# One product for two message parts, for two gathered tiles and for both supers of a pair, and a third part split by keys

## The reference: what is computed

```
h   = relu(layernorm(x))                      # 6250 x 64
msg = sum over r of (etype == r) * (h[src] @ weight[r])
out = x + segment_sum(msg, dst, 6250)
```

## Time and profile before

| | us |
|---|---|
| median of 3 runs (1139.3 to 1141.56) | 1141.29 |
| the profiled execution's own time | 1139.6 |
| its span, first to last instruction | 1137.9 |
| PE busy | 1105.6 (97%) |
| DVE busy | 982.7 (86%) |
| POOL busy | 712.3 (63%) |
| ACT busy | 498.1 (44%) |

### The profile page before, as it was taken

One profiled execution on the slowest core, in us unless ns is written; L12 is line 12 of the kernel. 1 busy time (PEld: TensorE's weight loads), 2 busy tenths in 40 slices (PEclk: granted clock), 3 DMA queues, 4 the chain that ended last, 5 costly groups with the idle time before them and its releaser, 6 DMA issues.

```text
span 1137.9 us, 41624 instructions
## 1 busy us (share of the span) xinstructions
PE 1105.6 (97%) x16806; PEld 689.4 (61%) x16806; DVE 982.7 (86%) x2609; ACT 498.1 (44%) x1227; POOL 712.3 (63%) x696
## 2 busy tenths in 40 slices
PE   3899999999999999999999999999999999999996
PEld 1444666666666666666666666666666666666664
DVE  7965798898898889988998998988998899899973
ACT  4866444443444344434443444434443444344441
POOL 1410577777666766777676677776666776776730
PEclk9989999999999999999999999999999999999999
DMA  6876422122222221222122221222122222221211
GB/s 187 346 282 245 159 85 77 58 84 84 78 58 84 81 85 57 78 84 84 56 79 83 84 77 60 84 82 81 57 83 83 82 59 80 79 86 60 77 46 58
DMA packets 40043, 108.99 MB, mean 96 GB/s; under 512 B 15917, under 2 KB 15919, under 8 KB 36780
## 3 DMA queue, kind: packets, MB, share of 16 engines
q1 hardware_dynamic: 13566, 55.53, 13.8%
q0 software_dynamic: 21344, 21.90, 8.2%
q10 hardware_dynamic: 4942, 28.88, 6.4%
HBM read 78.56 MB, written 27.70 MB: 93 GB/s over the span
## 4 chain that ended last, share of the span: by engine, by line
PE 94%; DMA 2%; ACT 2%; DVE 1%; issue 0%; POOL 0%; SPq 0%; ACTq 0%; DVEq 0%; POOLq 0%
PE ps L1045 50%; PE ps L1030 25%; PE ps L1067 5%; PE ps L1081 4%; PE ps L942 3%; PE ps L975 3%; PE ps L969 1%; PE ps L983 1%; PE ps L989 1%; DMA w_cat<-weight 1%; ACT u L546 1%; DVE h_sb L906 1%; DMA table<-u 1%; ACT vals L528 0%; PE ps L936 0%
## 5 line engine op out<-in xcount | busy, mean ns | idle before, releaser
L475 POOL DMA_INDIRECT u<-table,row_idx x667 | 689.4, 1034 | 344.5 <-PE ps L1045 176.5
L1045 PE MATMUL ps<-u 64*64 64x512 bf16 x9600 | 587.3, 379 | 0.0
L592 ACT CAST u<-ps 128x384 bf16<-128x384 f32 (+1 forms) x832 | 339.1, 473 | 440.9 <-PE ps L1030 433.6
L783 DVE TENSOR_SCALAR u<-iota_key,z_sb 128x512 bf16<-128x512 f16 x1600 | 495.6, 380 | 24.2 <-PE ps L1045 22.2
L1045 PEld LDWEIGHTS ps<-u 64*64 64x64 bf16 x9600 | 255.2, 106 | 233.2 <-issue 30.0
L1030 PE MATMUL ps<-parts,u 128*128 128x192 bf16 x3136 | 314.6, 247 | 0.8 <-ACT u L546 0.8
L1030 PEld LDWEIGHTS ps<-parts,u 128*128 128x128 bf16 x3136 | 249.5, 98 | 64.9 <-issue 56.5
L773 DVE TENSOR_SCALAR u<-u,node_id 128x1664 bf16<-128x1664 f16 (+2 forms) x256 | 162.7, 676 | 8.6 <-DMA u<-rel_dram 8.6
L803 DVE TENSOR_TENSOR accT<-accT,ps 128x32 f32 x240 | 44.8, 186 | 61.9 <-DVE accT L803 24.2
L601 ACT COPY u<-ps 128x512 f32<-128x512 f32 x128 | 68.8, 590 | 39.6 <-PE ps L1045 39.6
L732 DVE TENSOR_TENSOR u<-iota_slot,rank 128x896 f16<-128x896 f16 x64 | 70.0, 1094 | 2.2
(11 more groups left out here) (90 smaller groups left out, 365.7 us busy)
## 6 DMA issues: line engine op xcount, KB each, us to landing
u<-rel_dram SPq DMA_DIRECT2D x64, 800.0 KB
table<-u ACTq DMA_DIRECT2D x24, 1024.0 KB, 5.2
u<-table,row_idx POOLq DMA_INDIRECT x667
rel_dram<-rel_row SPq DMA_DIRECT2D x64, 6.2 KB
x_sb<-x SPq DMA_DIRECT2D x2, 448.0 KB
out<-h_sb SPq DMA_DIRECT2D x3, 224.0 KB
out<-h_sb ACTq DMA_DIRECT2D x3, 224.0 KB
table<-u ACTq DMA_DIRECT2D x1, 512.0 KB, 3.3
```

The lines of the kernel that those rows point to most:

```text
L475: pool.indirect_dma_start(out=msg_p[:, b, j, :], out_offset=None, in_=table, in_offset=bass.IndirectOffsetOnAxis(ap=row_idx[:, j, m:m + 1] ...
L592: act.copy(msg_s[:, u % MB, 0:width, :].rearrange("p q c -> p (q c)"), ps[gather_bank(u)][:, 0:width * ROW]).then_inc(s_gev, 1)
L783: dve.tensor_scalar(khot[:, v % KR, :], iota_key[:, :], z_sb[:, n % 3, 1, q:q + 1], None, ALU.is_equal).then_inc(s_khot, 1)
L1045: last = pe.matmul(ps[3 + a][half * D:(half + 1) * D, :], msg_s[rows, u % MB, q % 2, part * D:(part + 1) * D], khot[rows, v % KR, :], star ...
```

## The change

Four edits, of which the first three join products on PE:

1. `sum_sorted`: parts 0 and 1 of a range are one product with a stationary operand of 64 slots x 128 features (64*128), for each super. Part 2 stays 64*64: for a bank of two ranges four products, as before. For the lone range part 2 is split by keys: 256 keys to the one half, 256 to the other, so four products of 256 columns stand for two of 512.
2. `sum_gathered`: two tiles are one product of 128 edges x 128 (two tiles of 64) by 64 columns (two windows of 32), all 128*128. Only the two diagonal blocks of the result are used, so DVE adds each block's sum in two pieces of 64 rows (`add`), and the places in the bank are twice as wide.
3. `sort_permute`: both supers' slots are one stationary operand of 128 columns, 7 products of 100 columns instead of 14 of 50. ACT takes the two diagonal blocks in two copies, and DVE writes the slots' one-hot in the new order (`placed`).
4. The planner's cost of a lone range's sums goes from 2 to 1.5 rounds. The sums of gathered blocks stay where they are in PE's stream; for some tiles the PE event after which POOL fetches is another one close by.

```diff
@@ -147 +148 @@
             now += 0.14
             last_n, last_c = STREAM[i - 1]
             for b in banks_of(last_n, last_c):
-                now += 0.214 * (3 if 2 * b + 1 < SQ else 2)
+                now += 0.214 * (3 if 2 * b + 1 < SQ else 1.5)
                 marks.append((now, "agg", last_n * SQ + min(2 * b + 2, SQ)))
         now += 0.72 * (c == 0 and n > T_PAIRS)
         for us, job, which in ((0.32, permuted, "z"), (0.13, turned, "relT"), (0.7, ranked, "ranked")):
@@ -179 +180 @@
 
     batch = [place[m] // 2 for m in range(NP)]
     batches = [[m for m in range(NP) if batch[m] == k] for k in range(NPR // 2 + 1)]
-    adds_of = lambda k: GR * (k >= 1) + len(batches[k])
+    adds_of = lambda k: GR * (k >= 1) + sum(min(2, len(tiles_of(m))) for m in batches[k])
     added_by = lambda k: sum(adds_of(i) for i in range(k + 1))
 
     def target_bank(k):
         return ps[(7, 5)[k % 2]]
 
     def sum_place(m):
-        at = GR * SW + batches[batch[m]].index(m) * PW
-        return slice(at, at + PW)
-
-    assert GR * SW + max(len(ms) for ms in batches) * PW <= BANK and max(len(ms) for ms in sums_in) <= len(sum_at)
+        at = GR * SW + batches[batch[m]].index(m) * 2 * PW
+        return slice(at, at + 2 * PW)
+
+    assert GR == 4 and GR * SW + max(len(ms) for ms in batches) * 2 * PW <= BANK and max(len(ms) for ms in sums_in) <= len(sum_at)
 
 
     def gather_bank(u):
@@ -272 +273 @@
         a0 += MB * ROW
         agg = u2[:, a0:a0 + GR * KEYS].rearrange("p (s c) -> p s c", s=GR)
         a0 += GR * KEYS
-        slot_hot = u2[:, a0:a0 + PT * CAP // 2].bitcast(F16).rearrange("p (c z) -> p c z", z=CAP)
+        slot_hot = u2[:, a0:a0 + PT * CAP // 2].bitcast(F16).rearrange("p (j z) -> p j z", j=SJ)
 
 
         u3 = sb("u3", [P, TRING * 2 * RD])
@@ -554 +555 @@
                 if g >= 3:
                     act.wait_ge(s_khot, (g - 2) * SQ)
                     act.wait_ge(s_relT, g - 2)
-                act.copy(z_sb[:, g % 3, :, :].rearrange("p v q -> p (v q)"), ps[6][:, 0:2 * SQ]).then_inc(s_zev, 1)
+                for a in range(2):
+                    rows = slice(a * CAP, (a + 1) * CAP)
+                    act.copy(z_sb[rows, g % 3, :, :].rearrange("p v q -> p (v q)"),
+                             ps[6][rows, a * 2 * SQ:(a + 1) * 2 * SQ]).then_inc(s_zev, 1)
 
             def take_rel(g):
                 act.wait_ge(s_relT, g + 1)
@@ -720 +724 @@
                 qids = qid_t[:, 2 * g:2 * g + 2, :].rearrange("p s j -> p (s j)")
                 dve.tensor_tensor(ranges[:, :, :], spread(qids, SQ), repeat(iota_range[:, :], PT), ALU.is_equal).then_inc(s_ranges, 1)
 
+            def placed(hots, first, ranks, n):
+
+                there = hots[:, :, :].rearrange("p j (a z) -> p a j z", a=2)
+                places = iota_slot[:, first:first + n].rearrange("p (a j z) -> p a j z", a=1, j=1).to_broadcast([P, 2, SJ, n])
+                mine = ranks.rearrange("p (a j z) -> p a j z", j=SJ, z=1).to_broadcast([P, 2, SJ, n])
+                return dve.tensor_tensor(there, places, mine, ALU.is_equal)
+
             def sort_slots(g):
 
                 dve.wait_ge(s_ranked, g + 1)
@@ -729 +740 @@
                 step(dve.tensor_reduce(rank[:, g, :], ranks[:, :, :], AX, ALU.add))
                 if g >= 1:
                     dve.wait_ge(s_z, g)
-                dve.tensor_tensor(slot_hot[:, :, :], repeat(iota_slot[:, 0:CAP], PT), spread(rank[:, g, :], CAP),
-                                  ALU.is_equal).then_inc(s_slots, 1)
+                placed(slot_hot, 0, rank[:, g, :], CAP).then_inc(s_slots, 1)
 
             def sort_values(g):
                 if g == 0:
@@ -775 +785 @@
                 last.then_inc(s_hot, 1)
 
             def key_hots(n, low, high):
-                dve.wait_ge(s_zev, n + 1)
+                dve.wait_ge(s_zev, 2 * (n + 1))
                 for q in range(low, high):
                     v = n * SQ + q
                     if v >= KR:
@@ -796 +806 @@
 
                 bank = target_bank(k)
 
-                def add(rows, base, width, at):
+                def add(base, *places):
+
                     if added[0]:
                         dve.wait_ge(s_add, added[0])
-                    here = accT[rows, bass.ds(base, width)]
-                    dve.tensor_tensor(here, here, bank[rows, at], ALU.add).then_inc(s_add, 1)
-                    added[0] += 1
+                    for rows, at in places:
+                        here = accT[rows, bass.ds(base, at.stop - at.start)]
+                        dve.tensor_tensor(here, here, bank[rows, at], ALU.add).then_inc(s_add, 1)
+                        added[0] += 1
 
                 if k == 1:
                     dve.wait_ge(s_acc0, 8)
@@ -821 +833 @@
                         base_row[0:1, NS + batches[k][0]:NS + batches[k][-1] + 1], engines=[dve.engine], min_val=0, max_val=N,
                         skip_runtime_bounds_check_because="the bases are clamped to it where they are made")
                     for m, base in zip(batches[k], bases):
-                        add(slice(0 if len(tiles_of(m)) > 1 else tiles_of(m)[0] % 2 * D, P), base, PW, sum_place(m))
+                        at = sum_place(m).start
+                        add(base, *[(slice(half * D, (half + 1) * D), slice(at + half * PW, at + (half + 1) * PW))
+                                    for half in range(0 if len(tiles_of(m)) > 1 else 1, 2)])
 
             dve.wait_ge(s_turn_s, 6)
             source_hots(0, 0)
@@ -978 +992 @@
             def sort_permute(g):
                 pe.wait_ge(s_slots, g + 1)
                 pe.wait_ge(s_vals, g + 1)
+
+                values = spreadv[:, :, :, :].rearrange("p (a j) v q -> p a j (v q)", j=SJ)
                 for j in range(SJ):
-                    for a in range(2):
-                        last = pe.matmul(ps[6][a * CAP:(a + 1) * CAP, 0:2 * SQ], slot_hot[:, a * SJ + j, :],
-                                         spreadv[:, a * SJ + j, :, :].rearrange("p v q -> p (v q)"), start=j == 0, stop=j == SJ - 1)
+                    last = pe.matmul(ps[6][:, 0:4 * SQ].rearrange("p (a c) -> p a c", a=2), slot_hot[:, j, :], values[:, :, j, :],
+                                     start=j == 0, stop=j == SJ - 1)
                 last.then_inc(s_z, 1)
 
             def sort_turn(g):
-                pe.wait_ge(s_zev, g + 1)
+                pe.wait_ge(s_zev, 2 * (g + 1))
                 pe.transpose(ps[6][0:SQ, 0:P], z_sb[:, g % 3, 0, :], ident[:, :]).then_inc(s_relT, 1)
 
             piece(0)
@@ -1038 +1053 @@
                 if n >= 1 and c == 0:
                     pe.wait_ge(s_aev, 2 * n)
 
-                def sums(q, part, half):
+                def sums(q, first, last, half, keys=slice(0, KEYS), stop=False):
                     u, v = n * GB + q // 2, n * SQ + q
                     for a in range(2):
                         rows = slice(a * CAP, (a + 1) * CAP)
-                        last = pe.matmul(ps[3 + a][half * D:(half + 1) * D, :], msg_s[rows, u % MB, q % 2, part * D:(part + 1) * D],
-                                         khot[rows, v % KR, :], start=q == 0 and part < 2,
-                                         stop=(q, part) in ((SQ - 1, 1), (SQ - 1, 2)))
-                    return last
+                        done = pe.matmul(ps[3 + a][half * D:(half + last - first) * D, keys],
+                                         msg_s[rows, u % MB, q % 2, first * D:last * D], khot[rows, v % KR, keys],
+                                         start=q == 0 and first == 0, stop=stop)
+                    return done
 
                 for b in banks_of(n, c):
                     both = range(2 * b, min(2 * b + 2, SQ))
                     pe.wait_ge(s_gev, n * GB + b + 1)
                     for q in both:
                         pe.wait_ge(s_khot, n * SQ + q + 1)
-                        sums(q, 0, 0)
-                        sums(q, 1, 1)
-                    for q in both:
-                        sums(q, 2, q % 2).then_inc(s_agg, 1)
+                        sums(q, 0, 2, 0)
+                    if len(both) == 2:
+                        for q in both:
+                            sums(q, 2, 3, q % 2).then_inc(s_agg, 1)
+                    else:
+                        sums(q, 2, 3, 0, slice(0, KEYS // 2), True)
+                        sums(q, 2, 3, 1, slice(KEYS // 2, KEYS), True).then_inc(s_agg, 1)
 
             def weigh(g):
                 k = g + 1
@@ -1075 +1093 @@
                 pe.wait_ge(s_gp[m % PRING], 16 * fetched(m))
                 if added_by(batch[m] - 2) > 0:
                     pe.wait_ge(s_add, added_by(batch[m] - 2))
-                tiles = tiles_of(m)
-                for j in tiles:
-                    rows, half = rows_of(m, j), j % 2
-                    last = pe.matmul(target_bank(batch[m])[half * D:(half + 1) * D, sum_place(m)], msg_p[rows, m % PRING, j, :],
```

(16 more changed lines are left out.)

## The result

The changed kernel takes 1321.9 us, median of 4 runs (1320.7 to 1322.54), against 1140.99 us for the kernel before in the same sitting: a ratio of 1.1587, 95% interval [1.1567, 1.1607]. It is slower by 180.9 us. The profiled execution took 1320.7 us with a span of 1318.9.

What follows compares the result with a forecast made beforehand. PE was taken to bound the kernel (97% busy, 94% of the chain). 1139.6 + 145.6 (sum_sorted) + 37.4 (sum_gathered) + 0 (sort_permute, fetches) = 1322.6, taken as 1319 us for rounding; range 1272 to 1365.

Steps and rivals of the forecast that it cites:

- The three terms: sum_sorted on PE: lone range's half round -6.9 us, changes into 64*64 +61.0, changes into 64*128 +91.5; together +145.6.
- the unknown one: sum_sorted: 832 new changes into 64*128 bf16 sums, taken at 0.11 us each, +91.5 us; bounds nothing and 0.20 each.
- the 58 ns between the means of the fp32 loads: sum_gathered: fp32 loads of 128 columns against 64 (195, 137 ns) pace the passes, 0.66 us a block instead of 0.35.
- the third rival: sum_sorted: wide 64-row bf16 loads are slow like L942's, 0.20 us into each 64*128 group; 1394 to 1398 us, chance 0.08.
- up to 36 was allowed for the adds: DVE: 111 more adds at 0.32 us from start to start, +36 us on an engine with 155 us to spare.
- 3.6 for rounding: Forecast's sum: 1322.6 lowered to 1319 us, since prices come from two-decimal rows; 0.005 less on each of 1340 is 7.
- The second: PE's changes of shape: one costs only where the row split changes; 1170 us, chance 0.05.
- The fourth: sum_gathered: the fp32 loads are hidden or no slower, so that edit costs nothing; 1282 us, chance 0.10.
- the fifth: sum_sorted: the two wide products don't run side by side, 1600 rounds more, +346; 1665 us, chance 0.02.
- The first: PE's small products: paced by the instruction, changes without a late producer free; 1114 us, faster, chance 0.04.

Runs made afterwards that it cites:

- e6: All sums 64*128, the second range's part 2 left out and the first range's part 1 added twice, against the kernel before: 1133.52 us, ratio 0.9943.
- e5: Only the sum_sorted edit, but in each chunk all 64*128 products first, then all 64*64, against the kernel before: 1167.0 us, ratio 1.0239.
- e7: Only the sum_gathered edit, with 32 moving columns instead of 64 (second tile's own sums left out), against the kernel before: 1182.71 us, ratio 1.0376.
- e4: Only the lone range's part 2 split by keys, all products 64*64, against the kernel before: 1301.04 us against 1293.09, ratio 1.005.
- e8: Only the sum_sorted edit, lone range's split included, run once more against the kernel before: 1300.14 us against 1291.3, ratio 1.0068.
- e2: Only the sum_gathered edit, in the first sitting, against the kernel before: 1282.01 us against 1293.09, ratio 0.9892.
- e3: Only the sort_permute edit (both supers in one product of 128 columns) against the kernel before: 1282.95 us against 1293.09, ratio 0.9894.
- e9: Only the sum_gathered edit, all 64 moving columns, run once more against the kernel before: 1281.67 us against 1291.3, ratio 0.9922.
- e11: The sum_gathered and sort_permute edits together, sums as before, against the kernel before: 1278.95 us against 1291.3, ratio 0.9898.
- e10: Only the lone range's part 2 split by keys, run once more against the kernel before: 1299.75 us against 1291.3, ratio 1.0059.
- e12: Lone range's split, and four chunks instead of five from the third pair on, sums 64*64, against the kernel before: 1301.06 us against 1290.94, ratio 1.0064.

## Why the prediction was right

It gave 1319 us with a range of 1272 to 1365; 1321.9 was measured.

**The bound** is PE before and after: the chain's 94% and 95%.

**Edit 1** was put at +145.6. By the chain a pair past the second takes 3 x 0.56 + 0.34 + 0.23 = 2.25 more, x 62 = 139.5, and the first two pairs about 4 more at the same prices: 143.5. The three terms: the rounds stay (e6: 2.05 against 2.07 for nine), so does the price of a change into 64*64; the unknown one, into 64*128 bf16, was taken as 0.11 and is 0.105 by e6. That it is a change of shape which costs, and not a slow wide product, is shown by e5: the same products, 0.46 us less a chunk with four changes fewer. The loads show what the time is: no load is made ahead over the change. By the Trainium skill's rule in "TensorEngine Tiling (Array Packing)", Key Properties, a change of mode drains the array; the trace agrees, with 0.115 us, and also where only the column width changes within 64 rows.

**Edit 2** was put at +37.4: measured 0.33 a block x 111 = 36.6. The term's reason, the 58 ns between the means of the fp32 loads, is borne out by e7, where half the moving columns left 1.46 of 1.48 us. It rests on something that the prediction didn't say: before, the two loads of a pair ran side by side, so a pair cost the time of one load. The Trainium skill's figure for a load in "TensorE: Matmul & The Clock Gate", LDWEIGHTS, about 107 ns for 128 columns by estimate, fits this pace of 0.11 a pass; for wide bf16 loads the trace denies it (mean 94 against 103 for the narrow ones). That was the third rival, and it fell: the pieces of 64*128 take 0.53 us, not 0.63.

**Edit 3** was put at nothing: +0.09 x 64 and -0.11 x 63 are -1.2. ACT's two copies were covered; DVE's busy time rose by 17 us where up to 36 was allowed for the adds.

**Edit 4** left nothing to see on the chain, and was not run alone.

The terms as measured add to 143.5 + 36.6 - 1.2 = 178.9, the spans differ by 1318.9 - 1137.9 = 181.0. Added over the whole chain, the sums are 144.2 longer, the gathered sums 36.7, the permute 6.1, the gather 7.7 shorter, together 179.3; the rest lies in pieces of the other engines. The forecast was 179.4 above before, 183.0 less 3.6 for rounding. That it came so near is in part luck: its terms were 4 too high (edit 1 by 2, edits 2 and 3 by 1 each), the 3.6 is about half of the 7 that it gave for rounding, with no reason for that half, and the 2 us of the other engines were in no term.

**The rivals.** The second (no cost within one row split) would have shown 0.43 for the first piece; it takes 0.53, and the chain's 2.63 for three banks is 3 x (0.105 + 0.12) + 9 x 0.216 = 2.62. The fourth (hidden fp32 loads) and the fifth (wide products one after another, 0.97 for the first piece) are excluded by 1.48 and 0.53. The first, time by the instruction, is wrong for this comparison, and e6 shows it: half as many products in each bank, 0.02 us a chunk. In the other sittings the ratios went its way in sign.

## What to carry to other kernels

Where PE's stream has no gaps, count the changes of array shape in its order, not the instructions: here each cost 0.105 to 0.12 us, half a round of 512 columns, so joining two products can pay only if their neighbours have the joined shape too. Even then it was worth little here: with every sum joined (e6) the time fell by 6.7 us of 1140, since the narrow products had run side by side already. A wider fp32 stationary operand made the load longer (137 to 191 ns for 64 to 128 columns), and where few columns were moved the load set the pace. The chain of a profile, with groups of different length of the same line, gives the price of a column and of a change apart by two subtractions.

## What the runs showed of the hardware that was not expected

In three sittings the same kernel before took 1291 to 1293 us. Each of the four sittings was on another chip (14, 10, 5 and 15; only the second was without it), so chip and time can't be told apart. PE's groups had gaps that no semaphore explains. Weight loads of e4, whose stretch shows the pattern (columns: start, length, group, idle before):

```profile
334.19 0.57 PEld L1045 LDWEIGHTS ps<-u 64*64 64x64 bf16 x14 [0.16 <-issue]
335.10 0.13 PEld L1045 LDWEIGHTS ps<-u 64*64 64x64 bf16 x3 [0.34 <-issue]
335.84 0.15 PEld L1045 LDWEIGHTS ps<-u 64*64 64x64 bf16 x3 [0.60 <-issue]
336.11 0.78 PEld L1085 LDWEIGHTS ps<-u 128*64 128x64 f32 x24
```

Within one group of the same shape nothing is issued for 0.60 us. How many instructions PE got can be read from the busy times by stretch; first the kernel before, whose only trace is one of 1139.6 us (PE and PEld, each with its count), then e4:

```profile
300.00:1000.00 700.00, 700.00 (x11260) 444.09 (x11258) 630.08 (x1723) 295.44 (x743) 495.40 (x478) 1.00 0.24 76
```

```profile
300.00:1100.00 800.00, 752.16 (x11138) 470.76 (x11141) 610.92 (x1684) 287.62 (x724) 472.74 (x469) 0.98 0.23 66
```

Products and loads together are 22518 / 700 = 32.2 per us before, and 22279 / 800 = 27.8 in e4. In e8, which needs fewer, the chain is nearly whole again: its share of "issue" is 1% against 5% in e4. The ratios of all nine runs have the sign that goes with that: what has fewer PE products than the kernel before (e2, e3, e9, e11) is 0.8 to 1.1% faster, what has more (e4, e10, e12) 0.5 to 0.6% slower, and edit 1, which pays 144 us elsewhere, only 0.6 to 0.7% slower, since it needs 18% fewer products. So under this condition PE seems to be held back by the supply of its instructions. That is not shown, and it isn't one fixed rate: in the same stretch e9 had gaps at 27.0 per us and e11 at 26.3, and e8, with 22.7, was still 15 us above its expected 1285. The granted clock doesn't explain it: the runs of the kernel before in e8's sitting had 0.980 to 0.991, against 0.994 to 0.998 in e5's, under 2% for a time that is 13% longer; e4 and e10 had 0.977, e8 0.995. What sets the condition was not tested, and the changed kernel as a whole was not run under it.
